# A gated cross-attention and FFN block on one core: another order for the first group and for the end

## The reference, cut to what matters

```python
q = layernorm(x) @ Wq.T + bq
k = ctx @ Wk.T + bk
scores = where(mask, -inf, q @ k.T)            # 128x128 for each batch
x1 = x + tanh(g_xattn) * (softmax(scores) @ ctx @ Wo.T + bo)
w = where(w_ffn >= 0, 1.0, -1.0)
y = clip(layernorm(x1) @ w.T * scale + bias, -100, 100)
out = x1 + tanh(g_ffn) * y
```

## Time and profile before

| | |
|---|---|
| median of three runs | 83.41 us |
| profiled execution, its own time | 82.64 us |
| its span, first to last instruction | 80.9 us |
| TensorE busy | 68.2 us (84% of the span) |
| VectorE / ScalarE / GpSimd busy | 58.8 / 44.5 / 53.1 us |
| mean granted TensorE clock | 0.972 |
| start of K(0) / start of O(0) | 11.60 / 20.02 us |
| start of Z(1), start of Z(2) | 22.99 / 30.23 us |
| last instruction on VectorE ends | 78.74 us |

### The profile page before, as it was taken

One profiled execution on the slowest core, in us unless ns is written; L12 is line 12 of the kernel. 1 busy time (PEld: TensorE's weight loads), 2 busy tenths in 40 slices (PEclk: granted clock), 3 DMA queues, 4 the chain that ended last, 5 costly groups with the idle time before them and its releaser, 6 DMA issues.

```text
span 80.9 us, 1584 instructions
## 1 busy us (share of the span) xinstructions
PE 68.2 (84%) x507; PEld 63.1 (78%) x507; DVE 58.8 (73%) x185; ACT 44.5 (55%) x118; POOL 53.1 (66%) x108
## 2 busy tenths in 40 slices
PE   2977869936999999999999999999999999985200
PEld 2965659924999899989999998999999899744100
DVE  0038369373494797999799989979967996269990
ACT  0602094749189729936980995498289714713000
POOL 5400434899849758995998699589959077965420
PEclk9999999999999999999999999999999999999855
DMA  2799933999930000030003002100300040030123
GB/s 11 217 308 282 316 138 135 356 369 349 329 120 0 0 8 4 0 129 9 0 0 130 0 0 91 47 0 0 130 0 0 2 129 7 0 134 0 40 93 127
DMA packets 8288, 8.10 MB, mean 100 GB/s; under 512 B 596, under 2 KB 8152, under 8 KB 8280
## 3 DMA queue, kind: packets, MB, share of 16 engines
q1 hardware_dynamic: 7664, 7.47, 28.2%
q10 hardware_dynamic: 552, 0.53, 2.1%
q0 software_dynamic: 64, 0.00, 0.1%
HBM read 5.90 MB, written 2.10 MB: 99 GB/s over the span
## 4 chain that ended last, share of the span: by engine, by line
PE 64%; DMA 13%; DVE 8%; SPq 6%; ACT 4%; issue 2%; DVEq 0%
PE ps_Z L557 13%; DMA x_sb<-in_x_dram 13%; PE ps_K L557 12%; PE ps_O L628 9%; PE ps_F L557 8%; PE ps_S L557 8%; PE ps_xT L552 8%; PE ps_cT L552 3%; ACT p_sb L210 2%; PE ps_S L620 2%; DVE y_clip L455 1%; SPq L141 1%; SPq L144 1%; DVE y_scaled L446 1%; DVE x_sb L423 1%
## 5 line engine op out<-in xcount | busy, mean ns | idle before, releaser
L199 ACT ACTIVATE K_sb<-ps_K,u_col 128x256 f32<-128x256 f32 x16 | 6.7, 470 | 14.2 <-PE ps_K L557 14.2
L321 POOL TENSOR_TENSOR xb_sb<-x_sb,bo_g 128x256 f32<-128x256 f32 x16 | 11.4, 733 | 0.6
L326 POOL TENSOR_TENSOR y_biased<-y_scaled,bias_g 128x256 f32<-128x256 f32 x14 | 10.0, 736 | 2.5 <-DVE y_scaled L467 2.5
L557 PE MATMUL ps_K<-cT_hi,wqk_hi 128*128 128x256 f32 x32 | 10.4, 325 | 0.8 <-DVE wqk_lo L496 0.8
L557 PE MATMUL ps_Z<-woT_hi,cT_hi 128*128 128x256 f32 x32 | 9.8, 305 | 0.0
L557 PE MATMUL ps_Z<-woT_hi,cT_lo 128*128 128x256 f32 x32 | 9.0, 282 | 0.0
L557 PE MATMUL ps_K<-cT_lo,wqk_hi 128*128 128x256 f32 x32 | 9.0, 282 | 0.0
L557 PE MATMUL ps_K<-cT_hi,wqk_lo 128*128 128x256 f32 x32 | 9.0, 282 | 0.0
L557 PE MATMUL ps_Z<-woT_lo,cT_hi 128*128 128x256 f32 x32 | 9.0, 282 | 0.0
L189 ACT ACTIVATE xn<-x_sb,nmr_x,rstd_x 128x256 f32<-128x256 f32 x16 | 8.8, 607 | 0.0
L557 PE MATMUL ps_F<-wT,x1T_hi 128*128 128x256 f32 x30 | 8.1, 303 | 0.8 <-DVE x1T_lo L439 0.8
(11 more groups left out here) (114 smaller groups left out, 196.4 us busy)
## 6 DMA issues: line engine op xcount, KB each, us to landing
ctx_sb<-in_ctx_dram SPq DMA_DIRECT2D x8, 256.0 KB, 7.6
x_sb<-in_x_dram SPq DMA_DIRECT2D x8, 256.0 KB, 7.7
out_dram<-out_sb SPq DMA_DIRECT2D x7, 256.0 KB, 2.5
wk_sb<-in_L_xattn_Wk_dram ACTq DMA_DIRECT2D x1, 256.0 KB, 4.3
wq_sb<-in_L_xattn_Wq_dram SPq DMA_DIRECT2D x1, 256.0 KB, 4.0
wo_sb<-in_L_xattn_Wo_dram ACTq DMA_DIRECT2D x1, 256.0 KB, 7.2
mask_u<-in_mask_BxS_bk_dram SPq DMA_DIRECT2D x1, 256.0 KB, 7.9
w_sb<-in_L_ffn_weights_dram SPq DMA_DIRECT2D x1, 256.0 KB, 8.1
```

The costliest lines, as they stand in the source:

```text
L199: nc.scalar.activation(K_sb[:, g % 2, m], ps_K[:, m], ACT.Identity, bias=u_col[:, m:m + 1]).then_inc(K_done, 1)
L321: nc.gpsimd.tensor_tensor(xb_sb[:, r], x_sb[:, r], bo_g[:], ALU.add).then_inc(xb_done, 1)
L326: nc.gpsimd.tensor_tensor(y_biased[:, g % 2, b], y_scaled[:, g % 2, b], bias_g[:, 0], ALU.add).then_inc(biased_done, 1)
L557: last = nc.tensor.matmul(dst, lhsT, rhs, start=(n == 0), stop=(n == len(pairs) - 1))
```

## The change

**Head.** TensorE's first work is six matmuls of a tile of zeros that VectorE sets, in place of 18 transposes, and two more stand behind the transpose of the bias vectors. Wk is loaded from SyncE's list, second; the gates are loaded from ScalarE's, ahead of Wo; ctx(1) and the mask are loaded ahead of x(1), and x(2) and ctx(2) ahead of scale and bias. tanh stands ahead of the first copy of ctx on ScalarE. `wqk` goes to two banks, each copied by itself; the two halves of K(0) go to two banks. GpSimd, not ScalarE, normalises x(0); VectorE, not ScalarE, copies its transpose.

**Order of the first two groups.** TensorE takes the transposes of ctx(1) and S(0) ahead of Z(0). `w_mid` is transposed in group 1, no longer in group 0, and F(0) stands behind the transposes of x(2).

**End.** On ScalarE the exponentials of group 7 stand ahead of the copy of Z(7). On TensorE F(6) stands ahead of the second half of Z(7). The bias of F(6) is added on VectorE and its clip done on GpSimd; both biases of group 7 are added on VectorE; the two reciprocals are taken ahead of both x1.

The diff, cut to what bears on the order:

```diff
-WARM_UP = 18
+WARM_UP = 6
...
+        ps_wqk = [s[:, 0:D] for s in s_banks]
+        ps_K0 = [ps_K[:, 0], f_bank[:, 0:T]]
...
             sp.dma_start(wq_sb[:], wq.rearrange("(c p) d -> p c d", p=P)).then_inc(wq_loaded, 16)
+            sp.dma_start(wk_sb[:], wk.rearrange("(c p) d -> p c d", p=P)).then_inc(wk_loaded, 16)
             load_ctx(0)
             load_x(0)
-            load_x(1)
             load_ctx(1)
...
-            act.dma_start(wk_sb[:], wk.rearrange("(c p) d -> p c d", p=P)).then_inc(wk_loaded, 16)
             for k, v in enumerate((bq, bk)):
                 act.dma_start(vec_rows[k * DC:(k + 1) * DC, :], v.rearrange("(c p) -> c p", p=P)).then_inc(vecs_loaded, 16)
+            for k, v in enumerate((g_xattn, g_ffn)):
+                act.dma_start(gates[:, k:k + 1], v.rearrange("(o d) -> o d", o=1).to_broadcast([P, 1])
+                              ).then_inc(gates_loaded, 16)
             act.dma_start(wo_sb[:], wo.rearrange("(c p) d -> p c d", p=P)).then_inc(wo_loaded, 16)
...
-            normalise_x(0)
             act.wait_ge(u_ready, 1)
-            evict_K(0)
-            evict_xT(0)
+            for m in range(DC):
+                act.wait_ge(ps_K0_ready, m + 1)
+                nc.scalar.activation(K_sb[:, 0, m], ps_K0[m], ACT.Identity, bias=u_col[:, m:m + 1]).then_inc(K_done, 1)
+            evict_cT_hi(1)
+            normalise_x(1)
+            exp(0)
+            evict_PT(0)
             evict_Z(0)
+            evict_xT(1)
...
+                elif i == L:
+                    exp(i)
+                    evict_Z(i)
...
             norm_of_x(0)
+            pool.wait_ge(nmr_x_done, 1)
+            for b in range(GB):
+                nc.gpsimd.tensor_scalar(xn[:, b], x_sb[:, b], rstd_x[:, b:b + 1], nmr_x[:, b:b + 1],
+                                        ALU.mult, ALU.add).then_inc(xn_done, 1)
...
+            dve.wait_ge(xT_prod, 1)
+            nc.vector.tensor_copy(xT[:, 0], ps_xT).then_inc(xT_done, 1)
             stats_x(1)
+            mask_and_min(0)
+            split_cT(1)
...
+            residual(0)
+            stats_x1(0)
             dve.wait_ge(w_mean_ready, 1)
             for c in range(DC):
                 nc.vector.tensor_scalar(w_mid[:, c], w_sign2[:, c], w_mean[:, c:c + 1], None, ALU.subtract
                                         ).then_inc(w_mid_ready, 1)
+            stats_x(2)
...
-            clip_and_add(L - 1)
+            dve.wait_ge(pool_clip_done, 2 * GB)
+            nc.vector.tensor_tensor(out_sb[:, rows(L - 1)], y_clip[:, (L - 1) % 2], x1_sb[:, rows(L - 1)], ALU.add
+                                    ).then_inc(out_done, 1)
...
+            pe.wait_ge(zeros_ready, 1)
+            for _ in range(WARM_UP):
+                nc.tensor.matmul(f_bank[:, 0:P], zeros[:], zeros[:], start=True, stop=True)
             pe.wait_ge(ident_ready, 1)
-            for _ in range(WARM_UP):
-                nc.tensor.transpose(f_bank[:, 0:P], ident[:], ident[:])
...
             project_K(0)
             transpose_x(0)
+            transpose_ctx(1)
+            scores(0)
             project_Z(0)
...
+            transpose_x(1)
+            transpose_p(0)
+            attend(0)
+            project_K(1)
+            transpose_x1(0)
+            project_Z(1)
+            scores(1)
+            transpose_ctx(2)
+            pe.wait_ge(w_mid_ready, DC)
+            transposes(ps_wT, w_mid).then_inc(ps_wT_ready, 1)
+            transpose_p(1)
+            transpose_x(2)
+            ffn(0)
+            attend(1)
...
             project_Z(L, [0])
             scores(L)
+            ffn(L - 1)
             project_Z(L, [1])
-            ffn(L - 1)
             finish_last()
```

More of the change, by code:

```diff
@@ L158, in _ @@
                          ).then_inc(bias_loaded, 16)
-            for g in range(2, G):
+            for g in range(3, G):
                 load_x(g)
@@ L269, in _ @@
                                     pattern=[[-1, P]], channel_multiplier=1).then_inc(ident_ready, 1)
-            for k, v in enumerate((g_xattn, g_ffn)):
-                pool.dma_start(gates[:, k:k + 1], v.rearrange("(o d) -> o d", o=1).to_broadcast([P, 1])
-                               ).then_inc(gates_loaded, 16)
             def norm_of_x(g):
@@ L367, in _ @@
                     norm_of_x(i + 2)
+                if i == 0:
+                    fold_affine()
+            pool.wait_ge(lim_ready, 2)
+            clip(L - 2)
+            add_x1(L - 2)
+            clip(L - 1)
+            for b in range(GB):
+                rstd_of_last_x1(b)
         @block.vector
@@ L492, in _ @@
                                         ).then_inc(wq_neg_ready, 1)
+            stats_x(0)
             split_cT(0)
-            stats_x(0)
-            dve.wait_ge(wqk_hi_ready, 1)
-            nc.vector.tensor_tensor(wqk_lo[:], ps_K, wqk_hi[:].bitcast(F32), ALU.subtract).then_inc(wqk_lo_ready, 1)
+            for m in range(DC):
+                dve.wait_ge(wqk_hi_ready, m + 1)
+                nc.vector.tensor_tensor(wqk_lo[:, m], ps_wqk[m], wqk_hi[:, m].bitcast(F32), ALU.subtract
+                                        ).then_inc(wqk_lo_ready, 1)
+            dve.wait_ge(ps_u_ready, 1)
+            nc.vector.tensor_copy(u_col[:], ps_u).then_inc(u_ready, 1)
             dve.wait_ge(woT_hi_ready, 1)
@@ L513, in _ @@
                                         ).then_inc(w_mid_ready, 1)
-            for i in range(G):
-                if i >= 1:
+            stats_x(2)
+            for i in range(1, G):
+                if i >= 2:
                     residual(i - 1)
                     stats_x1(i - 1)
-                if i + 2 < G:
+                if 2 <= i < G - 2:
                     stats_x(i + 2)
-                if i >= 1:
-                    split_x1T(i - 1)
-                if i < G:
-                    mask_and_min(i)
+                split_x1T(i - 1)
+                mask_and_min(i)
                 if 2 <= i < L:
@@ L527, in _ @@
                     split_cT(i + 1)
-                if i >= 1:
-                    scale_y(i - 1)
+                if i == 1:
+                    stats_x(3)
+                scale_y(i - 1)
+            dve.wait_ge(scaled_done, GB * L)
+            nc.vector.tensor_tensor(y_biased[:, (L - 1) % 2], y_scaled[:, (L - 1) % 2], bias_g[:].to_broadcast([P, GB, D]),
+                                    ALU.add).then_inc(dve_biased_done, 1)
+            for b in range(GB):
+                r = L * GB + b
+                dve.wait_ge(p_done, r + 1)
+                nc.vector.reciprocal(recip_p[:, r:r + 1], psum_p[:, r:r + 1]).then_inc(recip_done, 1)
             for b in range(GB):
@@ L677, in _ @@
             for m in range(DC):
-                last = accumulate(ps_K[:, m], [(wk_sb[:, e, m * P:(m + 1) * P], wq_neg[:, e]) for e in range(DC)])
-            last.then_inc(ps_wqk_ready, 1)
+                accumulate(ps_wqk[m], [(wk_sb[:, e, m * P:(m + 1) * P], wq_neg[:, e]) for e in range(DC)]
+                           ).then_inc(ps_wqk_ready, 1)
             pe.wait_ge(wo_loaded, 16)
@@ L688, in _ @@
             transpose_x(0)
+            transpose_ctx(1)
+            scores(0)
             project_Z(0)
-            for i in range(L):
-                if i >= 1:
-                    project_K(i)
-                if i >= 1:
-                    transpose_x1(i - 1)
-                if i >= 1:
-                    project_Z(i)
+            transpose_x(1)
[12 more added lines that the diff above has]
+            attend(1)
+            for i in range(2, L):
+                project_K(i)
+                transpose_x1(i - 1)
+                project_Z(i)
                 scores(i)
                 transpose_ctx(i + 1)
-                if i >= 1:
-                    ffn(i - 1)
-                else:
-                    pe.wait_ge(w_mid_ready, DC)
-                    transposes(ps_wT, w_mid).then_inc(ps_wT_ready, 1)
+                ffn(i - 1)
                 transpose_p(i)
```

113 lines of the change are left out of this document (56 added, 57 removed).

## The result

The changed kernel takes **89.15 us** (median of 4 executions, 88.79 to 90.48), the kernel before on the same chip 83.75 (83.16 to 85.63): a ratio of **1.0655**, with an interval of 1.0534 to 1.0776. It is slower, as forecast, but by 5.40 us where 3.3 were forecast (6.6%, not 4%); 89.15 stands at the very top of the range of 84.3 to 89.2.

The account below looks back on a forecast made before the run. TensorE's work bounds the middle, so only head, first passage and end can move: -0.6 + 0.2 + 3.5 + 0.7 - 0.5 = +3.3 us, 85.9 against the profiled 82.64, forecast median 86.7 us; 8-in-10 range 84.3 to 89.2.

Parts of the forecast that it names:

- From O(0) to O(1): First passage, counted from O(0) as A: exponentials wait for nmr_x of x(2), F(0) for wT; +3.5 us (+2.5 to +4.2).
- The clock: TensorE's gaps ahead of O(0) and O(1): half of one fall to the lower level, +0.7 us (bounds 0 and 2.9).
- From K(0) to O(0): Counted from K(0) as T: wait for nmr_x of x(1) replaces that for x(2); +0.2 us (-0.6 to +0.8).
- Start of K(0): Head: K(0) at 11.0, not 11.60, behind Wo's rows; -0.6 us (-1.8 to +1.0), near 12.6 with a slow clock.
- a sign of being wrong: Head: the changed profile should show u, not wqk_lo, as the step before K(0), at 10.9 to 11.3.
- The middle: Groups after O(1): statistics run two groups ahead again, period stays 7.24 us; change 0.
- The end: Behind K(7): O(7) within 0.1 us of before, VectorE loses a clip and a reciprocal, adds biases; -0.5 us (-0.9 to 0).
- the cover that I named and dropped: End: GpSimd's extra work is hidden while it waits for VectorE; otherwise late rstd holds the last scaling by up to 0.7 us.
- Two falls: Rival, both gaps ahead of O(0) and O(1) drop the clock: 2.9 in place of 0.7, +5.5, 88.9 us; chance 0.20.
- Wo was not early: Rival, head: Wo lands before 8.5, K(0) starts at 9.8, clock holds; +1.4, 84.8 us, within 2%; chance 0.14.
- the third: Rival, head: gates late again, tanh at 9.7 puts K(0) back to 11.6 and above; +3.9, 87.3 us; chance 0.10.
- Nothing was faster: Rival, first passage: no wait for nmr_x of x(2), head's gain kept; -0.9, 82.5 us at most; chance 0.05.

Follow-up runs that it names:

- second execution: The unchanged changed kernel, profiled again beside the first experiments: 87.93 us, set against the 82.64 of before.
- stats_early: The changed kernel with the statistics of x(1) ahead of the copy of xT and those of x(2) ahead of w_sign: 85.24 us, ratio 1.0236.
- before_late: The kernel before with only the statistics of x(2) moved behind x1 of group 0 and its statistics: 82.57 us, ratio 1.0007.
- gates_pool: The changed kernel with the two gate transfers issued by GpSimd again: 89.84 us, ratio 1.0846.
- warm_more: The changed kernel with ten zero matmuls in place of two behind the transpose of the bias vectors: 88.62 us, ratio 1.0644.
- first execution: The first profiled execution of the changed kernel, the longest of its four: 90.48 us.
- stats_oldtail: stats_early with the whole end of the kernel before: 85.17 us, with the kernel before there at 83.22.

## Why the prediction was right or wrong

In the second execution the forecast fell short by 1.97 us: 0.46 at the start of K(0), 0.36 from there to O(0), 0.54 in the middle, 0.27 + 0.41 at the end, and -0.07 from O(0) to O(1). The median of the change stands another 1.22 above that execution. The step that is off most is the start of K(0), which had 0.46 in this execution and 3.74 in the other.

**From O(0) to O(1): right.** Forecast 3.5 for the waits and 0.7 for the clock, together 4.2; measured 4.13. With A at 20.44, `nmr_x` was done at A+6.05 (forecast A+6.25), the exponentials began at A+7.55 (A+7.85), F(0) at A+9.52 (A+9.7) and O(1) at A+11.37 (A+10.75). The small steps were shorter by 0.2 to 0.3, and F(0) cost 0.83 more at the lower level. stats_early removes the wait for `nmr_x` of x(2), and 3.02 of the 4.13, by moving two calls, and before_late makes the wait appear by moving one: this cause is shown. The transposes of `w_mid`, which the forecast left out of "the same pieces as before", were hidden by the wait.

**The clock: one fall, at a lower price.** The forecast priced a fall at 1.45 and took half of one. Each of the four profiles with this order (both executions, gates_pool, warm_more) had one fall around O(1), none had two. In the second execution it came in the second gap and cost 0.83, on F(0). In the first it came during O(0) (1.47 us, not 1.13), and there it cost only 0.34: K(1) and the transposes behind it ran slowly where TensorE would have waited anyway. In gates_pool it came at the start of O(0):

```profile
21.62 2.08 PE L666 MATMUL ps_O<-Z_sb,PT_sb 128*128 128x256 f32 x4 [0.84 <-ACT Z_sb L210]
```

That O(0) took 0.95 longer, the statistics waited for it, and the passage took 11.49. So a fall ahead of a wait is paid only for the work that the wait's own chain needs. The Trainium skill, in TensorE: Matmul & The Clock Gate, under HAM oscillation, has the clock fall in waits between bursts. For the second gap the trace of the second execution agrees (1.00, then 0.53). For the first gap only one execution agrees: TensorE was busy 1.32 us of 3.50 there in both, and the clock fell behind it in the first execution and not in the second.

**From K(0) to O(0): mechanism right, size small.** +0.56, not +0.2. The statistics of x(1) began at T+2.95 (forecast T+2.80), `nmr_x` was ready at T+5.85 (T+5.55) and the exponentials began at T+6.89 (T+6.55). VectorE's copy of `xT` started at T+2.34, not T+2.11, and GpSimd's `mr_x` took 0.45 us where it took 0.19 before.

**Start of K(0): the step that failed.** The forecast had the products end at 9.0, the clock of the warm-up as a mere bound, and 11.0 as the start, "as the nearest rows are those of Wo". It was 11.46 in one execution and 14.74 in the other, outside the bound of 12.6. The premise that failed is that the loads behind Wk on SyncE's queue would be there in time: the forecast priced Wk's move only by what it did for Wo, and its cost for ctx(0) and x(0) at nothing. In the first execution ctx(0) landed at 8.7 in place of 5.7, the products behind that gap took 3.62 us, and `u` was the step ahead of K(0), as forecast. In the second `wqk_lo` was, which the forecast named as a sign of being wrong, and what held it was x(0). The change also swaps two calls on VectorE:

```diff
+            stats_x(0)
             split_cT(0)
-            stats_x(0)
```

so the low parts are queued behind the statistics of x(0), and x(0) landed at 9.09, 6.87 us behind its issue:

```profile
9.11 0.75 DVE L395 BATCH_NORM_STATS2 bn_x<-x_sb 128x6 f32<-128x256 f32 x2 [3.83 <-DMA x_sb<-in_x_dram]
...
9.99 0.66 DVE L410 TENSOR_TENSOR cT_lo<-ps_cT,cT_hi 128x512 fp32r<-128x512 f32 x1
10.57 0.75 DVE L514 TENSOR_TENSOR wqk_lo<-ps_S,wqk_hi 128x256 fp32r<-128x256 f32 x2
```

`wqk_hi` was complete at 9.74 and `u` at 11.04, so by these rows K(0) could have started near 11.04, the forecast's 11.0; that is an estimate, since no run undid the swap. Over all seven profiles with Wk ahead of ctx(0), K(0) started at 11.46 to 14.74 (middle value 12.83), and the products took over 3 us in five of them; with Wk on ScalarE's queue they did in three of ten. That explains most of why the median stands above the second profile's 87.93; that no other place varies as much I have from few profiles only.

**The middle: not 0 but +0.54.** The five periods took 7.61, 7.36, 7.34 and twice 7.36, where before has 7.25, 7.25, 7.30, 7.35 and 7.34: a passing cost of 0.36 and 0.11 in the first two, no slower pace. In the first, x1 of group 1 is late, and TensorE waits for it ahead of its transposes:

```profile
32.15 0.88 DVE L483 SCALAR_TENSOR_TENSOR y_scaled<-ps_F,rstd,scale_g 128x256 f32<-128x256 f32 x2 [1.21 <-PE ps_F L592]
32.94 0.16 DVE L428 RECIPROCAL recip_p<-psum_p 128x2 f32<-128x2 f32 x1
33.55 0.88 DVE L434 SCALAR_TENSOR_TENSOR x_sb<-ps_O,recip_p,xb_sb 128x256 f32<-128x256 f32 x2 [0.46 <-DVE recip_p L428]
```

x1 of group 1 starts 1.74 us behind O(1) (before: 1.24). F(0), waiting for the late `wT`, ends just ahead of O(1), so its scaling and the reciprocal are under way on VectorE until 33.10, when O(1) is done (32.99). For the 0.46 us behind that the profile names no other work, so this part of the cause is open, as is the 0.11 of the second period. stats_oldtail has 36.88 in this stretch too, so the tail has no part in it.

**The end: wrong in size, by the cover that I named and dropped.** Forecast -0.5 behind O(7), measured -0.09, and O(6) to O(7) 0.27 longer, not within 0.1. With F(6) ahead of the second half of Z(7) on TensorE, ScalarE is through with the exponentials and stands idle until Z(7) is done, and the copies of P are queued behind the copy of Z:

```profile
75.46 0.59 ACT L213 COPY Z_sb<-ps_Z 128x512 f32<-128x512 f32 x1 [0.89 <-PE ps_Z L592]
```

The rows of VectorE and then GpSimd at the end, which answer to the earlier trace rows:

```profile
79.58 0.68 DVE L571 TENSOR_TENSOR out_sb<-y_clip,x_sb 128x512 f32<-128x512 f32 x1
80.23 0.48 DVE L465 SCALAR_TENSOR_TENSOR y_scaled<-ps_F,rstd,scale_g 128x256 f32<-128x256 f32 x1
81.04 0.48 DVE L465 SCALAR_TENSOR_TENSOR y_scaled<-ps_Z,rstd,scale_g 128x256 f32<-128x256 f32 x1 [0.33 <-POOL rstd L310]
```
```profile
78.72 0.23 POOL L308 TENSOR_SCALAR ve<-mv 128x1 f32<-128x1 f32 x1 [1.11 <-DVE mv L453]
...
79.58 0.76 POOL L308 TENSOR_SCALAR ve<-mv 128x1 f32<-128x1 f32 x1
80.42 0.58 POOL L310 TENSOR_TENSOR rstd<-ve,minus_half 128x1 f32<-128x1 f32 x1
```

The clip is gone from VectorE, but the last `rstd` comes late and VectorE waits 0.33 for it. GpSimd's second `ve` took 0.76 us, the first 0.23. The prediction said that a late `rstd` would hold the last scaling, and costed it at nothing. By these rows the second scaling could have started at 80.62, 0.39 us behind the first as in the kernel before (75.56, then 75.95), in place of 81.04. That is an estimate of 0.42 us, with which the end would have come out at the forecast's -0.5.

**The rivals.** Two falls did not occur, though its 88.9 is nearest to the time: right number, other cause. Wo was not early in the change (its transposes began at 9.60). In gates_pool it was, landing near 7.4, and K(0) still started at 12.83, since the products ended at 11.75: ctx(0) and the clock decided, which this rival did not count. The gates were early, so the third fell. Nothing was faster, and stats_early shows why: with the wait gone the rest of the change still isn't below before.
